# Two MetaFormer layers with routed experts on one core: the last blocks of the expert loops written out behind the loops

## The reference

```python
x = x + _L0_conv_ref(_ln_c(x), L0_conv_W_qkv, L0_conv_W_proj, L0_conv_b_proj)
t = _to_tokens(x)
t = t + _L0_ffn_ref(_ln_t(t), L0_ffn_gate_w, ...)      # out += comb[:, e] * (silu(x @ w1[e] + b1[e]) @ w2[e] + b2[e])
x = _from_tokens(t, x)
x = x + _L1_conv_ref(_ln_c(x), L1_conv_W_qkv, L1_conv_W_proj, L1_conv_b_proj)
t = _to_tokens(x)
t = t + _L1_ffn_ref(_ln_t(t), L1_ffn_router_w, ...)    # out += cw[:, e] * ((a * silu(g)) @ W2[e] + b2[e])
```

## Time and profile before

| what | value |
|---|---|
| median of 3 timed runs | 615.0 us |
| lowest and highest of them | 613.79 and 617.75 us |
| the profiled execution | 618.2 us |
| its span, first to last instruction | 616.4 us |
| PE, PEld, DVE, ACT, POOL busy | 90%, 79%, 54%, 53%, 46% of the span |
| granted TensorE clock, mean of the span | 0.945 of full |

### The profile page before, as it was taken

How to read it: one execution, slowest core, us unless ns; L and a number is a source line. 1 busy time by engine, 2 the same in 40 slices (tenths; PEclk the granted TensorE clock), 3 DMA queues, 4 the chain that set the end, 5 groups by cost and what they waited for, 6 DMA issues and landing times.

```text
span 616.4 us, 15729 instructions
## 1 busy us (share of the span) xinstructions
PE 557.7 (90%) x3646; PEld 489.7 (79%) x3647; DVE 333.6 (54%) x755; ACT 327.6 (53%) x580; POOL 283.9 (46%) x346
## 2 busy tenths in 40 slices
PE   8999777999999999996959998689999999999962
PEld 4888536988999899996548775379999999999962
DVE  6657684455534555552176675734565565656430
ACT  5784304666655666663358722235666665665430
POOL 4675023454655465564426410414546555545431
PEclk9999869999999999998869996889999999999995
DMA  8442774446421552334342129432264555222120
GB/s 290 139 124 73 259 261 156 103 114 173 111 48 31 168 126 40 77 96 105 94 145 91 45 83 273 154 125 44 34 197 126 140 137 163 35 79 34 31 35 9
DMA packets 44698, 70.36 MB, mean 114 GB/s; under 512 B 5368, under 2 KB 36096, under 8 KB 44672
## 3 DMA queue, kind: packets, MB, share of 16 engines
q1 hardware_dynamic: 33728, 55.87, 28.4%
q0 software_dynamic: 10944, 14.17, 13.4%
HBM read 57.44 MB, written 13.63 MB: 115 GB/s over the span
## 4 chain that ended last, share of the span: by engine, by line
PE 69%; DVE 10%; DMA 7%; issue 5%; POOL 3%; ACT 2%; POOLq 1%; DVEq 1%; SPq 0%; ACTq 0%
PE banks L1144 15%; PE banks L1146 15%; PE banks L1145 15%; PE banks L1354 5%; PE banks L1175 5%; DMA expert_io<-xn_dram,gcol 3%; PE banks L1236 2%; PE banks L1323 2%; PE banks L1270 2%; DVE stats L822 2%; PE banks L1152 2%; DVE onehot_row L1009 2%; DMA out_dram<-expert_io,scol 1%; DMA mid_dram<-expert_io,scol 1%; PE banks L1259 1%
## 5 line engine op out<-in xcount | busy, mean ns | idle before, releaser
L1144 PE MATMUL banks<-w_hi,xT_hi 128*128 x336 | 120.5, 359 | 5.2 <-DVE xT_lo L1049 4.0
L1144 PE MATMUL banks<-w_hi,hT_hi 128*128 (+2 forms) x392 | 117.8, 301 | 6.7 <-DVE hT_lo L1106 6.7
L1146 PE MATMUL banks<-w_hi,xT_lo 128*128 x336 | 115.6, 344 | 0.0
L1145 PE MATMUL banks<-w_lo,xT_hi 128*128 x336 | 114.8, 342 | 0.0
L1146 PE MATMUL banks<-w_hi,hT_lo 128*128 (+2 forms) x392 | 112.7, 287 | 0.0
L1145 PE MATMUL banks<-w_lo,hT_hi 128*128 (+2 forms) x392 | 112.6, 287 | 0.0
L752 ACT COPY banks<-seed_rows 128x1024 f32 (+1 forms) x58 | 66.8, 1151 | 34.2 <-issue 13.9
L1144 PEld LDWEIGHTS banks<-w_hi,hT_hi 128*128 128x128 f32 (+2 forms) x392 | 76.6, 195 | 8.8 <-issue 7.2
L556 POOL TENSOR_TENSOR w_lo<-raw,w_hi 128x1024 fp32r<-128x1024 f32 (+1 forms) x24 | 58.7, 2468 | 44.4 <-ACT w_hi L632 44.4
L576 POOL DMA_INDIRECT expert_io<-xn_dram,gcol x56 | 56.8, 1015 | 45.7 <-POOL gcol L572 42.7
L1145 PEld LDWEIGHTS banks<-w_lo,hT_hi 128*128 128x128 f32 (+2 forms) x392 | 77.0, 196 | 0.0
(11 more groups left out here) (184 smaller groups left out, 896.3 us busy)
## 6 DMA issues: line engine op xcount, KB each, us to landing
raw<-in_L_ffn_w_dram SPq DMA_DIRECT2D x32, 512.0 KB, 4.2
raw<-in_L_ffn_W_dram SPq DMA_DIRECT2D x16, 672.0 KB, 4.1
raw<-in_L_ffn_W_dram SPq DMA_DIRECT2D x16, 336.0 KB, 4.0
seed_rows<-in_L_ffn_b_dram SPq DMA_DIRECT2D x8, 672.0 KB
seed_rows<-in_L_ffn_b_dram SPq DMA_DIRECT2D x8, 512.0 KB
xn_dram<-raw SPq DMA_DIRECT2D x6, 512.0 KB, 3.0
xres<-in_x_dram SPq DMA_DIRECT2D x3, 512.0 KB, 4.5
wqkv<-in_L_conv_W_qkv_dram SPq DMA_DIRECT2D x2, 768.0 KB, 7.6
```

The costliest lines, as they stand in the source:

```text
L1144: pe.matmul(out, hi, w_high, start=first, stop=False, skip_group_check=onto)
L1145: pe.matmul(out, hi, w_low, start=False, stop=False, skip_group_check=onto)
L1146: return pe.matmul(out, lo, w_high, start=False, stop=last, skip_group_check=onto)
```

## The change

The loops of ScalarE and VectorE stop one block earlier, that of GpSimd two (`lead`), and the missing steps are written out behind the loop with `ahead=False`: they do nothing for a next block. TensorE reads the two last expert numbers before its loop, drops x_transpose(blocks), and does four filler matmuls before the last second product. The last block's rows are written by VectorE into xg and scattered from there by `last_scatter`, with a column (gcol) of its own. In layer 1 SyncE waits for the last landing itself.

```diff
+            for n in range(lead, 0, -1):
+                step(blocks - n, ahead=False)
+            step(blocks, ahead=False, last=True)
...
-            sp.wait_ge(lay[1].moe_done, 1)
+            sp.wait_ge(lay[1].tab, 2)
+            sp.wait_ge(lay[1].added, 16 * block_count(sp))
+            sp.sem_inc(lay[1].moe_done, 1)
...
+                def last_scatter(b):
+                    pool.wait_ge(s.gathered, 16 * b)
+                    pool.tensor_copy(gcol[:, :], col(scatter_tab, b)).then_inc(s.scol, 1)
+                    pool.wait_ge(s.scol, b + 1)
+                    pool.wait_ge(s.e_sb, b + 1)
+                    pool.wait_ge(s.added, 16 * b)
+                    pool.sem_inc(rows_go, 1)
+                    pool.indirect_dma_start(out=acc, out_offset=bass.IndirectOffsetOnAxis(ap=gcol[:, :], axis=0),
+                                            in_=xg, in_offset=None, bounds_check=TOKENS - 1,
+                                            oob_is_err=False, compute_op=ALU.add).then_inc(s.added, 16)
+
+                def step(b, ahead=True, last=False):
+                    if ahead:
                         gather(b + 2)
-                    if after(b, 1):
+                    if last:
+                        last_scatter(b - 1)
+                    elif after(b, 1):
                         scatter(b - 1)
-                    if last:
+                    if last and L == 0:
                         pool.wait_ge(s.added, 16 * b)
-                        pool.wait_ge(s.gathered, 16 * b + 16)
                         pool.sem_inc(s.moe_done, 1)
...
-                        if L == 0 and j == 1:
+                        if L == 0 and j == 1 and ahead:
...
+                    if not ahead:
+                        return
...
+                        rows = xg if last else y_sb(b - 1)
...
                 blocks = block_count(pe)
+                e_old, e_last = expert_of(blocks - 2), expert_of(blocks - 1)
...
-                e_old, e_last = expert_of(blocks - 2), expert_of(blocks - 1)
-                x_transpose(blocks)
                 second_product(blocks - 2, e_old)
                 h_transpose(blocks - 1)
+                keep_busy(BUSY_LAST, 3)
                 second_product(blocks - 1, e_last)
```

More of the change, by code:

```diff
@@ L346, in block_loop @@
                 eng.wait_ge(tab, 3)
-            steps(eng, 2, 0, blocks, step)
-            step(blocks, last=True)
+            steps(eng, 2, lead, blocks, step)
+            for n in range(lead, 0, -1):
+                step(blocks - n, ahead=False)
+            step(blocks, ahead=False, last=True)
         def piece_range(eng, b):
@@ L1098, in tables, with step @@
                     return pieces
-                def step(b, last=False):
+                def step(b, ahead=True, last=False):
                     if after(b, 1):
@@ L1110, in step @@
                     if L == 0:
-                        pieces = tables(b, last)
+                        pieces = tables(b, ahead)
                     if L == 1 and not last:
```

28 lines of the change are left out of this document (13 added, 15 removed).

## The result

The changed kernel takes 609.4 (median of five runs, 608.45 to 609.54), the kernel before 617.2 (five runs, 613.79 to 618.01). The ratio is 0.987, with a 95% interval of 0.9845 to 0.9898: faster by 1.3%, 7.8 us. The forecast of 603.0 had asked for 12.05, and 609.4 lies above its range, which ended at 607.8.

A forecast was written before the change was run, and what follows sets the result against it. TensorE was taken as busy over most of the span, with waits only where layers end. Gains 5.9 (layer 1's tail), 4.4 (layer 0's) and 1.75 (end) sum to 12.05; from 615.0 that gives 603.0, range 599.5 to 607.8.

The forecast's parts named there:

- the chance of 0.9 for faster by over 1%: Whole kernel: the forecast and rivals 1 to 3 together; 1% is about 6.15 us.
- the end: After layer 1's last scatter: SyncE waits for the landing, GpSimd's 4.98 drain begins sooner; gain 1.75.
- tail of layer 1: Layer 1's last blocks: skipped passes and copy leave the path, last scatter starts at 602.0, not 607.88; gain 5.9.
- tail of layer 0: Layer 0's last blocks: the chain of scatter landings decides, last scatter starts at 294.5, not 298.89; gain 4.4.
- A drain of 6.7 or more: GpSimd's drain at the program's end: a stated sign of a wrong forecast, which expected it to last 5.
- the first rival: Program's end: the drain waits for the last landing, so its 1.75 is not gained; time 604.7, chance 0.2.
- The trace has one drain and can't exclude it: Program's end: a transfer in flight might lengthen the drain, the only way the end's gain could go below nothing.
- the third rival: Layer tails: clock falls anyway, or VectorE's skipped passes delay block 26; rider: clock shifts elsewhere; 604.6 to 606.7, chance 0.15.
- the three skipped passes were read while the matmuls ran: TensorE behind block 27's first product: skipped passes cost no wait; the 2.0 pause was put to two loads, 0.85 apart.
- The landing's price: Last scatters: each waits for the landing before, 3.8 to 3.9 from scatter start by the trace, against the skill's 2.3.
- What was costed at nothing: Before the expert loop: TensorE's two added loads, 1.7, covered by 2.2 of waiting for the gather; uncovered, 1.7 per layer.
- The fourth rival: Loop bodies move in a longer program, passes cost more; gain lost from 0.24 per pass, 623 at 0.4; chance 0.03.

The follow-up runs named there:

- e1: Changed kernel, but in layer 1 GpSimd again waits for the last landing and SyncE only for moe_done; 610.24, ratio 0.988.
- e5: Kernel before the change, with six chained GpSimd copies in layer 1 between the last scatter's landing and the drain; 618.79 in one run.
- e14: Changed kernel with eight unused gathers put into layer 0 ahead of its sorting; 617.43.
- e11: Changed kernel with own columns and row buffers for scatters 25 and 26 too, so their copies are made during the landing before; 606.14, ratio 0.979.
- e7: Kernel before the change, with only TensorE's two loads of the last expert numbers moved ahead of its expert loop; 615.65 in one run.
- e4: Changed kernel without the scatter of block 26 in either layer, the counts of landings one lower; 604.12, ratio 0.9775.
- e12: Changed kernel with own buffers for the last three scatters and two unused gathers behind GpSimd's loop in each layer; 610.5, ratio 0.987.
- e13: Changed kernel with four unused gathers, each waited for, put into layer 0 ahead of its sorting; 608.97.
- e6: Kernel before the change, with only VectorE's last step written out behind the loop; 613.99, ratio 0.994.
- e3: Changed kernel without the four filler matmuls before the last second product; 606.67, ratio 0.985.

## Why the prediction was wrong

The direction, and with it the chance of 0.9 for faster by over 1%, came out. The size did not. Between 603.0 and 609.4 lie 6.4, by these parts:

| part | share of the 6.4 |
|---|---|
| the median 615.0 of three runs, from which 12.05 was taken, was 617.2 over five | 2.2 |
| the end: 1.75 forecast, -0.4 measured | 2.1 |
| tail of layer 1: 5.9 forecast, 5.4 measured | 0.5 |
| tail of layer 0: 4.4 forecast, 5.3 measured | -0.9 |
| stretches that the change doesn't touch, between the two profiles | 1.3 |
| profile pair (9.0) against medians (7.8) | 1.2 |

**The step that failed is "The end".** "If it takes the same from the end of GpSimd's own 1.57 of scatter" was the condition, and the drain did not take the same: 7.11. "A drain of 6.7 or more" was among the forecast's own signs of being wrong. The hand-over's own part was sized nearly rightly (1.5 in e1 against the changed kernel). That the drain waits for no transfer is borne out by e5, and by the changed kernel and e1 together: 7.11 from the end of the scatter instruction with the transfer in flight, 7.10 with all landed. So the first rival is not what happened, though the profile alone would look like it: the end is later than forecast by about the amount which that rival had given. Its evidence would have been a drain that ends a fixed time behind the landing in e1 and in the changed kernel alike. In e1 it starts after the landing and still takes 7.10. "The trace has one drain and can't exclude it" named a bound below nothing, of a transfer in flight; the real one came with nothing in flight, and the range had no room for it. Why the drain of the changed program is 2.1 longer stays open.

**The base.** A difference worked out from a profile of 618.2 was taken from a median of 615.0 that stood on three runs between 613.79 and 617.75. Over five runs the median is 617.2, and beside the experiments it was 617.0 to 619.0 (with e14 and with e11). From 617.2 the same sum gives 605.2, and the range moved by the same 2.2 would end at 610.0, with the result just inside.

**Layer 1's tail** went as worked out, step by step. Counted from e_sb (25), forecast and measured: second product of block 26 at 4.17 and 4.55, transposes of h at 6.4 and 6.80, hT_lo (27) at 8.0 and 7.84, last product at 8.9 and 8.71, e_sb (27) at 11.5 and 11.24, scatter 26 at 8.9 and 9.41, last scatter at 13.7 and 14.12. The missing 0.5 is all in scatter 26, from which the last one follows as forecast (4.71 against 4.8): it is 0.54 late, 0.38 of that by the start of block 26's product, whose pause of 0.43 the forecast had at nothing. That pause is not the third rival's either. VectorE's skipped passes were covered with some 0.3 to spare: hT_lo (26) at 587.33 and the 0.86 of the forecast give 588.19, and the first product ended at 588.51. What the forecast had wrong is "the three skipped passes were read while the matmuls ran": TensorE reads the last of them as the product ends. e7 shows it alone, with hT_lo (26) early: the pause behind the first product is still 0.37. In layer 0 the cover was bare indeed, and TensorE waits 0.55 for hT_lo (26) at 282.90, but there the landings decide. The clock stayed up, as the forecast said.

**Layer 0's tail.** The last scatter was forecast at 294.5 and started at 294.28. It was bound, as said, by the chain of landings, and e_sb (27) at 291.35 was ahead of it. Of the 0.9 that the table credits, 0.68 is chance: e_sb (25) was that much later in this execution. By the clock of the profile the last scatter came 4.61 sooner, where 4.4 was forecast.

**The landing's price.** From a scatter's start to the next scol copy are 288.22 - 284.49 = 3.73 in layer 0, and in layer 1 590.30 - 586.47 = 3.83; the earlier trace rows had 3.93. The estimate of 2.3 by the Trainium skill, "DMA: Bandwidth & Descriptors", anatomy of one DMA, would have put e_sb on the path in both tails; e4 shows what that looks like, and the changed kernel doesn't. SyncE sees the last landing 3.1 behind the start of the scatter instruction and 1.5 behind its end, so the estimate fits neither count, and the rows decide.

**What was costed at nothing.** TensorE's two loads ahead of the loop cost nothing, as the forecast had it. TensorE does twelve filler matmuls while the first gather is under way, and in both layers the first transposes (L1323 before, L1342 after) follow them without a pause, with the loads and without:

```profile
394.19 3.40 PE L1152 MATMUL banks<-busy_in 128*128 128x512 bf16 x12
397.43 0.38 PE L1323 MATMUL banks<-ident,expert_io 128*128 128x128 f32 x2
```

```profile
391.11 4.15 PE L1171 MATMUL banks<-busy_in 128*128 128x512 bf16 x12
395.10 0.38 PE L1342 MATMUL banks<-ident,expert_io 128*128 128x128 f32 x2
```

The two new loads are done at 393.74. (In layer 0 of e12 and e13 there is a pause ahead of the transposes, 0.8 and 0.9, but the loads are done over a microsecond before its end.) The fillers themselves took 0.75 longer in the second profile, at a granted clock of 0.65 (391.10 to 395.10) against 0.80 (394.20 to 397.40). That is as much as the whole difference between the two profiles from layer 0's last scatter to layer 1's first e_sb (117.37 and 118.12), and part of the 1.3 of the untouched stretches. It is the rider of the third rival, a clock that rises at another place, though not shown to come from the change: this stretch is 114.65 to 117.37 in the three kernels without the loads (before, e5, e6) and 115.27 to 119.15 in the 17 with them. The rest of it is the 0.68 by which layer 0's e_sb (25) is later in the second profile. The fourth rival, a dearer loop pass, didn't happen: from layer 1's e_sb (0) to e_sb (25) are 172.07 before and 171.98 after.

## What to carry to other kernels

Where accumulating scatters must follow each other, work saved on the engines at a loop's end was worth here only as much as the chain of landings let through; look for what starts the scatter before the last, and put copies under its landing (e11). A fixed step at a program's very end that one profile shows is a number from one program, so a forecast that moves it should allow for another length (here 2.1 on 4.98). And the base of a forecast is the median of as many runs as there are, with its own uncertainty in the range: here it cost as much as the wrong step.

## What was not expected of the hardware

GpSimd's drain at the end of the program costs 4.98 to 5.15 or 6.94 to 7.22, begins when GpSimd reaches it, waits for no landing (e5, e1), and had the one or the other length in kernels that differ by harmless-looking edits to GpSimd's program: 2.1, over a quarter of what the whole change brought. TensorE's clock stayed at its upper level through a pause of 1.08 in front of the last product (e3), while behind the pause of 3.35 it had been at the lower one. Behind the pause of 2.0 it went both ways: in the profile before it is at 1.00 through the product of block 26 (594.4 to 597), in e5 and e6 it fell in it (0.57 in 592 to 596, 0.50 in 589 to 590). Four unused gathers with a wait after each, ahead of layer 0's sorting, left the time as it was within the interval (e13, 608.97), but eight delayed layer 0's first e_sb from 109.94 to 119.41 and cost the whole gain (e14, 617.43).
